# Filling TensorE's first waits with transposes of the identity, and reordering low parts, gathers and up products before the second sequence

## Chip, cores and metric

The kernel runs on one core of one Trainium2 chip. The metric is the device time of one execution in microseconds (us). The core has five engines with their own instruction streams: TensorE (PE; its weight loads are a row of their own, PEld), VectorE (DVE), ScalarE (ACT), GpSimd (POOL) and SyncE (SP, which only issues transfers). Engines wait for one another through semaphores.

## What is computed

The reference is one layer of a language model on 8 sequences of 512 tokens with 128 channels:

```python
h = concat(fine_embed[ids], softmax(cluster[ids] + b) @ coarse)          # token embedding
h = h + attn(layernorm(h))    # rms norm, linear attention with a decay mask, then a gelu "memory" step
h = h + ffn(layernorm(h))     # 2 shared and 64 routed experts, top 6 of 64 per token, 64 hidden units each
# an expert: silu(x @ gate.T) * (x @ up.T) @ down.T, times the token's gate value
```

A token past an expert's capacity gets a gate of zero there, so the kernel needs a running count over the tokens of all sequences.

## The kernel before

The work goes sequence by sequence (`BATCHES` = 8, called b), each in two parts. The first part (the *early* and *late* steps: embedding, attention, router) makes the normalised tokens x3 and the gates of a sequence. The second part runs all experts on all tokens, two experts at a time: `PAIRS` = 33 pairs, p = 0 to 32. For a pair, `gate_up` issues six matmuls of 128x512 (gate and up, each as hi*hi, hi*lo and lo*hi of weights split in two fp32r parts), ACT applies silu (`act_silu`), DVE multiplies by the up product (`dve_up`), POOL multiplies by the gates (L998, or L1002 for pair 0), and four pairs later `down` multiplies by the down weights into one PSUM bank. For odd pairs ACT and DVE also split the hidden values (`act_hi`, `dve_lo`).

The order on each engine is written out by hand. While the experts of sequence b run, the steps of sequence b+1 (late) and b+2 (early) are interleaved: the tables `PE_AT`, `DVE_AT`, `ACT_AT` and `POOL_AT` say at which pair p a step is issued. Before the first sequence nothing can be interleaved, so the same tables are run through without pairs: the *start* of the kernel is a chain of small steps that go from engine to engine. Its steps are: products of the small weights ("prep", L506 to L530), the coarse embedding of sequence 0 (L431, L437), transposes of xn (L343), y (L349 to L351), z and scores (L360 to L362), state (L370), mem (L378, L381), transposes of xn2 (L388), vals (L394), op (L400), transposes of x3 (L406), router logits (L411), the top 6 on DVE, and transposes of the gates (L419). Then DVE counts the tokens of each expert (L795), makes the gates (L800), and SP stores them to DRAM and reads them back as one row per expert, spread over 64 partitions (`gate_row_loads`, L293).

The expert weights come in six chunks of 11 pairs (`CHUNKS`); for each, ACT rounds to the hi part (`split_hi`) and DVE subtracts to get the lo part (`split_lo`, L272). The last number of a chunk's tuple says at which step DVE does it: below `PAIRS` in the start, from `PAIRS` on within the first sequence. `DOWN_LO_AT` is the same for the down weights (L277). Some buffers of later steps serve as staging for these chunks (`hid`, `gate_rows`, `later`).

Token rows are fetched by `gather` on POOL (indirect transfers): those of sequences 0 and 1 at the beginning, those of sequence b+2 between the pairs 1 to 4 of sequence b. `POOL_AT["hx"]` is an addition of 128x512 on POOL (L971) that DVE's h2 (L719) needs much later.

```python
for p in range(PAIRS):
    if p == PE_AT["gates_t"]:
        ...
        for k in range(AHEAD):
            gate_up(pe, 0, 0, k)
    pe_late(pe, 0, 0, p, False)
    pe_early(pe, 1, p - SHIFT, bank_y)
sequences(pe, lambda *a: pe_sequence(pe, *a))
```

Of the kernel before, what the change touches and what calls it, by code (L numbers as in the profile page):

```python
# [29 lines left out]
P = 128  # L30
BATCHES, SEQ = 8, 512
TILES = SEQ // P
# [15 lines left out]
SPLITS = PAIRS // 2  # L48
DOWN_HI_AT, DOWN_LO_AT = 10, PAIRS + 1

# [23 lines left out]
CHUNKS = (("gate", 0, "hid0", None, -20, 3),  # L74
          ("up", 0, "rows", None, -20, 10),
          ("gate", CHUNK, "hid1", None, 3, 14),
          ("up", CHUNK, "later", None, 5, 14),
          ("gate", 2 * CHUNK, "own0", None, 5, PAIRS + 6),
          ("up", 2 * CHUNK, "own1", None, 7, PAIRS + 9))
CHUNK_OF = {(n, p0): k for k, (n, p0, *_) in enumerate(CHUNKS)}  # L80
SHIFT = 3
AHEAD = 2


def build(nc, ids, table, coarse_w, square_w, small_cols, small_rows, gate_t, up_t, down_t, out):
    ctx = ExitStack()
    with ctx:
# [397 lines left out]
        def pe_sequence(pe, b, par, late, early):  # L485
            first = b == 0
            for p in range(PAIRS):
# [10 lines left out]
                if early:  # L498
                    pe_early(pe, b + 2, p)

        @block.tensor
        def _(pe):
            f0, f1 = bank_f

            pe.wait_ge(sem("squares"), 16)
            pe.matmul(f0[:, 0:P], small_w["q"][:, :], small_w["k"][:, :], start=True, stop=True)  # L506
            pe.matmul(f0[:, P:2 * P], small_w["v"][:, :], small_w["o"][:, :], start=True, stop=True,
                      skip_group_check=True)
            pe.matmul(f0[:, 2 * P:3 * P], small_w["read"][:, :], basis[:, :], start=True, stop=True,
                      skip_group_check=True)  # L510
            pe.matmul(f0[:, 3 * P:4 * P], small_w["write"][:, :], basis[:, :], start=True, stop=True,
                      skip_group_check=True).then_inc(sem("pe_prep"), 1)

            pe.wait_ge(sem("ident"), 2)
            pe.wait_ge(sem("powers"), 3)
            pe.transpose(bank_g[0][:, 0:P], mask_t[:, :], ident[:, :])
            pe.matmul(bank_g[0][:, P:2 * P], to_end[:, :], ident[:, :], start=True, stop=True, skip_group_check=True)
            pe.matmul(bank_g[0][:, 2 * P:2 * P + 1], powers_t[:, :], ident[:, 0:1], start=True, stop=True,
                      skip_group_check=True).then_inc(sem("pe_powers"), 1)
            pe.wait_ge(sem("prep1"), 1)  # L520
            pe.matmul(f1[:, 0:P], qk_in[:, :], basis[:, :], start=True, stop=True)
            pe.matmul(f1[:, P:2 * P], vo_in[:, :], basis[:, :], start=True, stop=True,
                      skip_group_check=True).then_inc(sem("pe_prep"), 1)
            pe.wait_ge(sem("coarse_w"), 16)
            for p in range(PAIRS):
                pe_early(pe, 0, p, bank_y)
            pe.wait_ge(sem("prep2"), 1)
            pe.matmul(f0[:, 0:P], qk_t[:, :], basis[:, :], start=True, stop=True, skip_group_check=True)
            pe.matmul(f0[:, P:2 * P], vo_t[:, :], basis[:, :], start=True, stop=True, skip_group_check=True)
            pe.matmul(f0[:, 2 * P:3 * P], read_s[:, :], small_w["mix"][:, :], start=True, stop=True,  # L530
                      skip_group_check=True).then_inc(sem("pe_prep"), 1)
            pe.wait_ge(sem("prep3"), 1)
            pe.wait_ge(sem("cols"), 16)
            for p in range(PAIRS):
                if p == PE_AT["gates_t"]:
                    pe.wait_ge(sem("x3_hi"), 1)
                    pe.wait_ge(sem("x3_lo"), 1)
                    for k in range(AHEAD):
                        gate_up(pe, 0, 0, k)
                pe_late(pe, 0, 0, p, False)  # L540
                pe_early(pe, 1, p - SHIFT, bank_y)
            sequences(pe, lambda *a: pe_sequence(pe, *a))
            last = BATCHES - 1
            for p in range(PAIRS - LAG, PAIRS):
                down(pe, last, 1, p)
            pe_out(pe, last)
# [315 lines left out]
        def dve_sequence(dve, b, par, late, early):  # L862
            first = b == 0
            for p in range(PAIRS):
# [6 lines left out]
                if first:  # L871
                    split_lo(dve, PAIRS + p)
                dve_up(dve, b, par, p)
                if p >= SPLIT_LAG and is_split(p - SPLIT_LAG):
# [5 lines left out]
        def _(dve):  # L880
# [57 lines left out]
            dve.wait_ge(sem("decays"), 3)  # L938
            for p in range(PAIRS):
                dve_late(dve, 0, 0, p)  # L940
                dve_early(dve, 1, 1, p - SHIFT, 1, bank_y)
                split_lo(dve, p)
# [18 lines left out]
        def pool_late(pool, b, par, p):  # L961
# [7 lines left out]
            if p == POOL_AT["hx"]:  # L969
                pool.wait_ge(sem("x2"), b + 1)  # L970
                pool.tensor_tensor(hx[:, :, :], emb[par][:, :, :], x2[:, :, :], ALU.add).then_inc(sem("hx"), 1)  # L971
# [10 lines left out]
        def pool_sequence(pool, b, par, late, early):  # L982
            for p in range(PAIRS):
                if late:
                    pool_late(pool, b + 1, 1 - par, p)
                if early:
                    pool_early(pool, b + 2, p)
                    if p in GATHER_AT:

                        gather(pool, b + 2, par, GATHER_AT.index(p))  # L990
# [15 lines left out]
        def _(pool):  # L1006
# [17 lines left out]
            for p in range(PAIRS):  # L1024
                pool_late(pool, 0, 0, p)
                pool_early(pool, 1, p - SHIFT)
            sequences(pool, lambda *a: pool_sequence(pool, *a))

# [50 lines left out]
```

## Time and profile before

| | us |
|---|---|
| median of 3 runs (lowest, highest) | 728.99 (728.93, 729.01) |
| the profiled execution, its own time | 728.14 |
| its span, first to last instruction | 726.3 |
| TensorE busy in the span | 683.9 (94%) |
| DVE / ACT / POOL busy | 525.2 / 349.5 / 464.8 |

The page shows engines' busy time, a strip of 40 slices of some 18 us each, the chain of work that ended last, and groups of instructions. TensorE's clock as granted is given in shares of full speed (1.00 is 2.4 GHz, 0.50 is 1.2 GHz). In the strip TensorE is below nine tenths only in the first five slices and in the last one:

```profile
PE   4547899999999999999999999999999999999997
PEclk8566999999999999999999999999999999999999
```

### The profile page before, as it was taken

The page shows a single profiled execution, that of the slowest core. Times are in us where ns is not written, and L with a number is a line of the kernel's source. Part 1 is how long each engine was busy: PE and PEld are TensorE (multiplying, and loading weights), DVE is VectorE, ACT ScalarE, POOL GpSimd, SP SyncE. Part 2 cuts the span into 40 slices and gives each one's busy share as a digit, 9 for nine tenths or more (in the row PEclk, how much of TensorE's full clock was granted, in tenths as well). Part 3 has the DMA queues.
Part 4 walks back from the last instruction along what each step waited for, and adds up shares of the span by engine and source line. Part 5 has one row for each costly group of instructions (what it writes and reads, how often), then busy time and mean ns, then how long its engine had stood idle before and what let it go on. Part 6 is the DMA issues. An engine that isn't in the chain of part 4 may idle for free.

```text
span 726.3 us, 9592 instructions
## 1 busy us (share of the span) xinstructions
PE 683.9 (94%) x2943; PEld 512.9 (71%) x2943; DVE 525.2 (72%) x1073; ACT 349.5 (48%) x607; POOL 464.8 (64%) x345
## 2 busy tenths in 40 slices
PE   4547899999999999999999999999999999999997
PEld 3426677777777777777777777777777777777775
DVE  4477877787769877788679877788678866674443
ACT  3333374545554474544654465533745445534432
POOL 5013667685676776676776856777676656676664
PEclk8566999999999999999999999999999999999999
DMA  5501333343333433333333433333334334444431
GB/s 202 221 1 44 112 102 99 116 120 105 116 102 94 131 103 102 116 116 110 109 110 95 131 98 106 115 115 109 107 99 118 115 98 115 107 118 122 138 122 55
DMA packets 48851, 80.14 MB, mean 110 GB/s; under 512 B 9504, under 2 KB 13728, under 8 KB 48800
## 3 DMA queue, kind: packets, MB, share of 16 engines
q1 hardware_dynamic: 47776, 77.44, 34.7%
q0 software_dynamic: 1024, 2.10, 1.4%
q8 instruction: 23, 0.38, 0.2%
q14 instruction: 28, 0.23, 0.1%
HBM read 76.35 MB, written 3.15 MB: 109 GB/s over the span
## 4 chain that ended last, share of the span: by engine, by line
PE 90%; DVE 4%; issue 1%; POOL 1%; ACT 1%; DVEq 0%; POOLq 0%
PE bank_y L459 16%; PE bank_g L473 8%; PE bank_u L475 8%; PE bank_g L475 8%; PE bank_u L474 8%; PE bank_u L473 8%; PE bank_g L474 8%; PE bank_y L454 4%; PE bank_y L456 4%; PE bank_y L453 4%; PE bank_f L378 1%; PE bank_f L394 1%; PE bank_f L411 1%; PE bank_f L400 1%; PE bank_f L370 1%
## 5 line engine op out<-in xcount | busy, mean ns | idle before, releaser
L998 POOL TENSOR_TENSOR hid<-hid,gate_rows 128x512 f32<-128x512 f32 x256 | 374.0, 1470 | 190.1 <-DVE hid L848 189.2
L596 ACT ACTIVATE hid<-bank_g 128x512 f32<-128x512 f32 x264 | 156.4, 598 | 268.2 <-PE bank_g L475 265.5
L848 DVE TENSOR_TENSOR hid<-hid,bank_u 128x512 f32<-128x512 f32 x264 | 178.5, 681 | 131.2 <-PE bank_u L475 78.3
L473 PE MATMUL bank_g<-x_hi,gate_hi 128*128 128x512 f32 x264 | 143.7, 544 | 0.0
L459 PE MATMUL bank_y<-hid,w_down 128*128 128x512 f32 x272 | 138.8, 592 | 0.0
L854 DVE TENSOR_TENSOR hid_lo<-hid,hid_hi 128x512 fp32r<-128x512 f32 x128 | 111.2, 869 | 1.6 <-ACT hid_hi L602 1.5
L475 PE MATMUL bank_g<-x_lo,gate_hi 128*128 128x512 f32 x264 | 105.4, 399 | 0.0
L475 PE MATMUL bank_u<-x_lo,up_hi 128*128 128x512 f32 x264 | 105.3, 399 | 0.0
L474 PE MATMUL bank_g<-x_hi,gate_lo 128*128 128x512 f32 x264 | 105.0, 398 | 0.0
L473 PE MATMUL bank_u<-x_hi,up_hi 128*128 128x512 f32 x264 | 105.0, 398 | 0.0
L474 PE MATMUL bank_u<-x_hi,up_lo 128*128 128x512 f32 x264 | 104.7, 397 | 0.0
L602 ACT ACTIVATE hid_hi<-hid 128x512 fp32r<-128x512 f32 x128 | 80.4, 628 | 5.6 <-POOL hid L998 5.2
L473 PEld LDWEIGHTS bank_g<-x_hi,gate_hi 128*128 128x128 f32 x264 | 50.6, 192 | 24.2 <-issue 19.2
L474 PEld LDWEIGHTS bank_g<-x_hi,gate_lo 128*128 128x128 f32 x264 | 50.7, 192 | 23.6 <-issue 19.2
L459 PEld LDWEIGHTS bank_y<-hid,w_down 128*128 128x128 f32 x272 | 51.2, 188 | 12.0
L474 PEld LDWEIGHTS bank_u<-x_hi,up_lo 128*128 128x128 f32 x264 | 50.1, 190 | 12.1
L473 PEld LDWEIGHTS bank_u<-x_hi,up_hi 128*128 128x128 f32 x264 | 50.2, 190 | 11.9
L475 PEld LDWEIGHTS bank_u<-x_lo,up_hi 128*128 128x128 f32 x264 | 50.0, 190 | 11.9
L475 PEld LDWEIGHTS bank_g<-x_lo,gate_hi 128*128 128x128 f32 x264 | 50.2, 190 | 11.6
L453 PE MATMUL bank_y<-hid_hi,down_hi 128*128 128x512 f32 x128 | 51.1, 399 | 0.0
L456 PE MATMUL bank_y<-hid_lo,down_hi 128*128 128x512 f32 x128 | 50.9, 398 | 0.0
L454 PE MATMUL bank_y<-hid_hi,down_lo 128*128 128x512 f32 x128 | 50.9, 398 | 0.0
(199 smaller groups left out, 828.1 us busy)
## 6 DMA issues: line engine op xcount, KB each, us to landing
gate_rows<-gates_dram SPq DMA_DIRECT2D x512, 128.0 KB, 2.9
w_down<-down_t_dram SPq DMA_DIRECT2D x3, 704.0 KB, 14.0
out_dram<-later SPq DMA_DIRECT2D x8, 256.0 KB, 3.0
hid<-gate_t_dram SPq DMA_DIRECT2D x2, 704.0 KB, 5.8
gates_dram<-gates_t SPq DMA_DIRECT2D x8, 128.0 KB, 2.2
gate_rows<-up_t_dram SPq DMA_DIRECT2D x1, 704.0 KB, 5.7
later<-up_t_dram SPq DMA_DIRECT2D x1, 704.0 KB, 8.6
raw<-gate_t_dram SPq DMA_DIRECT2D x1, 704.0 KB, 9.5
```

What stands on the lines that cost most here:

```text
L453: pe.matmul(y, down_hi[:, j, :], hid_hi[:, k, :], start=False, stop=False)
L454: pe.matmul(y, down_lo[:, j, :], hid_hi[:, k, :], start=False, stop=False)
L456: pe.matmul(y, down_hi[:, j, :], hid_lo[:, k, :], start=False, stop=False).then_inc(sem("down_done"), 1)
L459: pe.matmul(y, w_down[:, p, :], hid[:, slot(par, p), :], start=(p == 0), stop=(p == PAIRS - 1)).then_inc(sem("down_done"), 1)
L473: pe.matmul(o, w_hi[name][:, p, :], x3_hi[par][:, :], start=True, stop=False)
L474: pe.matmul(o, w_lo[name][:, p, :], x3_hi[par][:, :], start=False, stop=False)
L475: pe.matmul(o, w_hi[name][:, p, :], x3_lo[par][:, :], start=False, stop=True).then_inc(sem("pe_" + name), 1)
L596: act.activation(hid[:, slot(par, p), :], bank_g[(p + par) % 2][:, :], ACT.Silu).then_inc(sem("silu"), 1)
L602: act.activation(hid_hi[:, (p // 2) % SPLIT_RING, :], hid[:, slot(par, p), :], ACT.Copy)\
L848: dve.tensor_tensor(hid[:, s, :], hid[:, s, :], bank_u[(p + par) % 2][:, :], ALU.mult)\
L854: dve.tensor_tensor(hid_lo[:, k, :], hid[:, slot(par, p), :], hid_hi[:, k, :].bitcast(F32), ALU.subtract)\
L998: pool.tensor_tensor(hid[:, s, :], hid[:, s, :], gate_rows[:, row, :], ALU.mult)\
```

## The change

TensorE gets extra transposes of the identity (`warm`): each reads `ident` and writes a PSUM bank that nobody reads then. They stand behind steps of the start, in counts that a table gives (20 before anything else, then 2, 9, 4, 26 in the preparation, and 8, 12, 9, 7, 36, 3, 2, 24, 4, 20, 6 behind later steps), in front of the waits that follow these steps. The rest of the change is another order:

- DVE's lo parts: up chunk 0 at step 7 (was 10), gate chunk 1 at step 10 (was 14), up chunk 1 within the first sequence (pair 5; was step 14 of the start), down at step 14 of the start (was pair 1 of the first sequence), the last two chunks at pairs 9 and 12 (were 6 and 9).
- `AHEAD` 3: three pairs' gate and up products are issued ahead of the first sequence, the third behind the transposes of the gates. DVE multiplies pair 0 ahead of the count of tokens and pair 1 right behind the gates, before xn of sequence 1.
- POOL: the gathers of sequence 2 stand before the first sequence; hx of sequence 0 waits for xn2 instead of x2.

```diff
-DOWN_HI_AT, DOWN_LO_AT = 10, PAIRS + 1
+DOWN_HI_AT, DOWN_LO_AT = 10, 14
...
-          ("up", 0, "rows", None, -20, 10),
-          ("gate", CHUNK, "hid1", None, 3, 14),
-          ("up", CHUNK, "later", None, 5, 14),
+          ("up", 0, "rows", None, -20, 7),
+          ("gate", CHUNK, "hid1", None, 3, 10),
+          ("up", CHUNK, "later", None, 5, PAIRS + 5),
...
-AHEAD = 2
+AHEAD = 3
+WARM = {1: 8, 3: 12, 5: 9, 6: 7, 7: 36, 12: 3, 14: 2, 17: 24, 20: 4, PE_AT["gates_t"]: 6}
+WARM_START, WARM_PREP, WARM_EXP, WARM_COARSE, WARM_GATES = 20, (2, 9), 4, 26, 20
...
+        def warm(pe, bank, count):
+            for _ in range(count):
+                pe.transpose(bank[:, 0:P], ident[:, :], ident[:, :])
...
+            pe.wait_ge(sem("ident"), 2)
+            warm(pe, bank_u[1], WARM_START)
             pe.wait_ge(sem("squares"), 16)
...
+            warm(pe, bank_u[1], WARM_COARSE)
             pe.wait_ge(sem("prep3"), 1)
             pe.wait_ge(sem("cols"), 16)
             for p in range(PAIRS):
                 if p == PE_AT["gates_t"]:
                     pe.wait_ge(sem("x3_hi"), 1)
                     pe.wait_ge(sem("x3_lo"), 1)
-                    for k in range(AHEAD):
+                    for k in range(AHEAD - 1):
                         gate_up(pe, 0, 0, k)
+                    warm(pe, bank_y[1], WARM_GATES)
                 pe_late(pe, 0, 0, p, False)
+                if p == PE_AT["gates_t"]:
+                    gate_up(pe, 0, 0, AHEAD - 1)
                 pe_early(pe, 1, p - SHIFT, bank_y)
+                warm(pe, bank_y[1] if p >= PE_AT["gates_t"] else bank_u[1], WARM.get(p, 0))
...
             for p in range(PAIRS):
+                if p == DVE_AT["taken"]:
+                    dve_up(dve, 0, 0, 0)
                 dve_late(dve, 0, 0, p)
+                if p == DVE_AT["taken"]:
+                    dve_up(dve, 0, 0, 1)
...
             if p == POOL_AT["hx"]:
-                pool.wait_ge(sem("x2"), b + 1)
+                pool.wait_ge(sem("x2" if b else "xn2"), b + 1)
...
-                    if p in GATHER_AT:
+                    if p in GATHER_AT and b:
...
+            for t in range(TILES):
+                gather(pool, 2, 0, t)
             sequences(pool, lambda *a: pool_sequence(pool, *a))
```

Where the order moves, on the engines that wait or are waited for. In all rows the first column is the line (lines of the changed kernel are some 4 to 24 higher), and `x36` means 36 in a row.

TensorE between mem (L378, L381; now L382, L385) and the transposes of xn2 (L388; now L392), the last rows of mem included. Before:

```order
L378 MATMUL bank_f<-z,shared 128x128
L381 MATMUL bank_f<-turns 128x128
L378 MATMUL bank_f<-z,shared 128x128
L388 MATMUL bank_f<-ident,xn 128x128 x4
L394 MATMUL bank_f<-xn_t,read_mix 128x512
L431 MATMUL bank_y<-ident,lg 64x128 x4
```

and with the change:

```order
L382 MATMUL bank_f<-z,shared 128x128
L385 MATMUL bank_f<-turns 128x128
L382 MATMUL bank_f<-z,shared 128x128
L508 MATMUL bank_u<-ident 128x128 x36
L392 MATMUL bank_f<-ident,xn 128x128 x4
L508 MATMUL bank_u<-ident 128x128 x3
L398 MATMUL bank_f<-xn_t,read_mix 128x512
L435 MATMUL bank_y<-ident,lg 64x128 x4
```

36 transposes of the identity stand in the longest wait of the start, three more in the next one.

VectorE from the gates' last product (L786; now L805) on: the count and the gates (L795, L800; now L814, L819), the up products of the first pairs (L848; now L867), and the lo part of the down weights (L277). Before:

```order
L786 TENSOR_TENSOR turns<-turns 128x4x64
L795 SCALAR_TENSOR_TENSOR taken<-ones_row,bank_f 64x512
L800 SCALAR_TENSOR_TENSOR gates_t<-taken,bank_f 64x512
L664 TENSOR_SCALAR xn<-emb,mv,inv 128x128 x4
L848 TENSOR_TENSOR hid<-hid,bank_u 128x512
L277 TENSOR_TENSOR down_lo<-w_down,down_hi 128x2048
L848 TENSOR_TENSOR hid<-hid,bank_u 128x512
L679 TENSOR_TENSOR x_lo<-bank_f,x_hi 128x512
```

and with the change, with the stretch further on where the lo part of up chunk 1 now stands (L276):

```order
L805 TENSOR_TENSOR turns<-turns 128x4x64
L867 TENSOR_TENSOR hid<-hid,bank_u 128x512
L814 SCALAR_TENSOR_TENSOR taken<-ones_row,bank_f 64x512
L819 SCALAR_TENSOR_TENSOR gates_t<-taken,bank_f 64x512
L867 TENSOR_TENSOR hid<-hid,bank_u 128x512
L683 TENSOR_SCALAR xn<-emb,mv,inv 128x128 x4
L698 TENSOR_TENSOR x_lo<-bank_f,x_hi 128x512
...
L689 TENSOR_SCALAR x<-emb,mv,inv 128x128 x4
L694 TENSOR_SCALAR shared<-xn,decay_cols 128x384
L276 TENSOR_TENSOR up_lo<-later,up_hi 128x1408
L867 TENSOR_TENSOR hid<-hid,bank_u 128x512
```

The long subtraction L277 is gone from between the first pairs; one of 1,408 columns has come in at pair 5.

GpSimd at the beginning of the first sequence: the gathers (DMA emb), pair 0 (L1002; now L1026) and the products with the gate rows (L998; now L1022). Before:

```order
L979 TENSOR_TENSOR inv<-var,neg_half 128x8
L1002 TENSOR_SCALAR hid<-hid 128x512
L958 DMA emb<-table_dram,idx 128x128
L998 TENSOR_TENSOR hid<-hid,gate_rows 128x512
L958 DMA emb<-table_dram,idx 128x128
L998 TENSOR_TENSOR hid<-hid,gate_rows 128x512
```

and with the change:

```order
L1003 TENSOR_TENSOR inv<-var,neg_half 128x8
L982 DMA emb<-table_dram,idx 128x128 x4
L1026 TENSOR_SCALAR hid<-hid 128x512
L1022 TENSOR_TENSOR hid<-hid,gate_rows 128x512 x9
L990 TENSOR_SCALAR ms<-ss 128x4
L992 TENSOR_TENSOR inv<-ms,neg_half 128x4
```

The four gathers stand together, ahead of pair 0.

## Rows read from the trace of the kernel before

**Rows 1.** Windows: us, busy by engine (instructions), TensorE's granted clock, DMA share, GB/s.

```profile
20.00:30.00 10.00, 5.60 (x19) 4.18 (x19) 5.33 (x12) 5.13 (x6) 0.00 (x0) 0.50 0.78 322
...
80.00:90.00 10.00, 8.04 (x38) 6.23 (x37) 8.74 (x14) 1.72 (x4) 5.05 (x4) 0.83 0.30 86
...
300.00:700.00 400.00, 398.80 (x1727) 298.91 (x1726) 293.91 (x578) 195.94 (x346) 273.83 (x196) 1.00 0.38 112
```

**Rows 2.** Timeline of TensorE, start: start, length, what, [idle before, releaser].

```profile
20.75 1.08 PE L343 MATMUL bank_f<-ident,xn 128*128 128x128 f32 x4 [3.98 <-DVE xn L664]
23.34 0.76 PE L349 MATMUL bank_f<-x_hi,qk_hi 128*128 128x512 f32 x1 [1.50 <-DVE x_lo L679]
...
24.33 0.63 PE L351 MATMUL bank_f<-x_lo,qk_hi 128*128 128x512 f32 x1
26.93 0.55 PE L360 MATMUL bank_f<-vo_y_hi,x_hi 128*128 128x256 f32 x1 [1.97 <-DVE turns L685]
...
29.41 0.41 PE L362 MATMUL bank_f<-vo_y_lo,x_hi 128*128 128x256 f32 x1
...
33.35 0.46 PE L378 MATMUL bank_f<-z,shared 128*128 128x128 f32 x2 [1.24 <-DVE turns L702]
...
35.74 0.64 PE L378 MATMUL bank_f<-z,shared 128*128 128x128 f32 x2
41.94 1.11 PE L388 MATMUL bank_f<-ident,xn 128*128 128x128 f32 x4 [5.56 <-DVE xn L713]
...
46.59 1.51 PE L400 MATMUL bank_f<-write_w,vals 128*128 128x128 f32 x8
...
52.81 1.11 PE L406 MATMUL bank_f<-ident,xn 128*128 128x128 f32 x4 [3.69 <-DVE xn L736]
54.62 1.97 PE L411 MATMUL bank_f<-cols,xn_t 128*128 128x64 f32 x8 [0.69 <-ACT xn_t L576]
...
62.88 0.66 PE L419 MATMUL bank_f<-ident,turns 128*128 128x128 f32 x4 [1.38 <-DVE turns L786]
```

**Rows 3.** Timeline of TensorE, first and last of 12 in z of sequence 1.

```profile
77.66 0.36 PE L360 MATMUL bank_f<-vo_y_hi,x_hi 128*128 128x256 f32 x1 [0.46 <-DVE turns L685]
...
79.03 0.28 PE L362 MATMUL bank_f<-vo_y_lo,x_hi 128*128 128x256 f32 x1
```

**Rows 4.** Timeline of VectorE, start and first sequence.

```profile
9.99 0.49 DVE L808 TENSOR_TENSOR lg<-emb,rows 128x256 f32<-128x256 f32 x1 [0.51 <-DMA emb<-table_dram,idx]
...
40.01 1.87 DVE L713 TENSOR_SCALAR xn<-shared,inv 128x128 f32<-128x128 f32 x4 [1.32 <-POOL inv L968]
...
44.58 1.62 DVE L272 TENSOR_TENSOR up_lo<-later,up_hi 128x1408 fp32r<-128x1408 f32 x1
...
51.65 1.11 DVE L736 TENSOR_SCALAR xn<-h,mv,inv 128x128 f32<-128x128 f32 x4 [0.80 <-POOL inv L974]
...
56.17 0.16 DVE L840 TENSOR_SCALAR var<-mv 128x4 f32<-128x4 f32 x1
...
74.13 2.32 DVE L854 TENSOR_TENSOR hid_lo<-hid,hid_hi 128x512 fp32r<-128x512 f32 x1 [1.18 <-ACT hid_hi L602]
...
78.03 3.20 DVE L670 TENSOR_SCALAR x<-emb,mv,inv 128x128 f32<-128x128 f32 x4
```

**Rows 5.** Timeline of ScalarE, ahead of vals of sequence 0.

```profile
44.01 1.28 ACT L573 ACT_TABLE_LOAD   x1
```

**Rows 6.** Timeline of GpSimd, first pairs of sequence 0.

```profile
67.45 3.37 POOL L1002 TENSOR_SCALAR hid<-hid 128x512 f32<-128x512 f32 x1 [9.40 <-DVE hid L848]
71.00 1.09 POOL L958 DMA_INDIRECT emb<-table_dram,idx  x1 [0.18 <-issue]
72.12 1.31 POOL L998 TENSOR_TENSOR hid<-hid,gate_rows 128x512 f32<-128x512 f32 x1
```

**Rows 7.** The tile gate_rows, 60 to 90 us: its transfers (issue length in ns, from where to where) and landing.

```profile
L293 SPq DMA_DIRECT2D gate_rows<-gates_dram x20: 444/596/606, 67.8 to 89.5; - x20
...
DMA to landing us min/median/max: 2.7/3.1/3.5
```

More of the change, by code:

```diff
@@ L74 @@
 CHUNKS = (("gate", 0, "hid0", None, -20, 3),
-          ("up", 0, "rows", None, -20, 10),
-          ("gate", CHUNK, "hid1", None, 3, 14),
-          ("up", CHUNK, "later", None, 5, 14),
-          ("gate", 2 * CHUNK, "own0", None, 5, PAIRS + 6),
-          ("up", 2 * CHUNK, "own1", None, 7, PAIRS + 9))
+          ("up", 0, "rows", None, -20, 7),
+          ("gate", CHUNK, "hid1", None, 3, 10),
+          ("up", CHUNK, "later", None, 5, PAIRS + 5),
+          ("gate", 2 * CHUNK, "own0", None, 5, PAIRS + 9),
+          ("up", 2 * CHUNK, "own1", None, 7, PAIRS + 12))
 CHUNK_OF = {(n, p0): k for k, (n, p0, *_) in enumerate(CHUNKS)}
 SHIFT = 3
-AHEAD = 2
+AHEAD = 3
+WARM = {1: 8, 3: 12, 5: 9, 6: 7, 7: 36, 12: 3, 14: 2, 17: 24, 20: 4, PE_AT["gates_t"]: 6}
+WARM_START, WARM_PREP, WARM_EXP, WARM_COARSE, WARM_GATES = 20, (2, 9), 4, 26, 20
 def build(nc, ids, table, coarse_w, square_w, small_cols, small_rows, gate_t, up_t, down_t, out):
@@ L512, in _ @@
                       skip_group_check=True).then_inc(sem("pe_prep"), 1)
-            pe.wait_ge(sem("ident"), 2)
             pe.wait_ge(sem("powers"), 3)
@@ L519, in _ @@
                       skip_group_check=True).then_inc(sem("pe_powers"), 1)
+            warm(pe, bank_u[1], WARM_PREP[0])
             pe.wait_ge(sem("prep1"), 1)
@@ L523, in _ @@
                       skip_group_check=True).then_inc(sem("pe_prep"), 1)
+            warm(pe, bank_u[1], WARM_PREP[1])
             pe.wait_ge(sem("coarse_w"), 16)
@@ L526, in _ @@
                 pe_early(pe, 0, p, bank_y)
+                if p == PE_AT["exp_t"]:
+                    warm(pe, bank_u[1], WARM_EXP)
             pe.wait_ge(sem("prep2"), 1)
@@ L872, in dve_sequence @@
                     split_lo(dve, PAIRS + p)
-                dve_up(dve, b, par, p)
+                if p >= AHEAD - 1 or not first:
+                    dve_up(dve, b, par, p)
                 if p >= SPLIT_LAG and is_split(p - SPLIT_LAG):
```

## The prediction

> **What bounds the kernel now.** I read the windows of ten microseconds first. From 300 to 700 us TensorE is busy 398.80 of 400 us at granted clock 1.00; nothing in the change touches that stretch, so no gain or loss is to be had there. From 20 to 30 us it is busy 5.60 of 10 us, and its clock is 0.50, the 1.2 GHz level; from 80 to 90 us it still has 0.83 of full clock, that is some 3.4 us at half speed [rows 1]. So all that can move lies in the first 90 us. The timeline of TensorE there shows a chain: a few matmuls, then a wait with a named releaser on DVE or ACT, eight of them in the rows, from 0.69 to 5.56 us [rows 2]. The matmuls of the chain run at half speed because TensorE waits so much, and each is waited for: its length is on the path. VectorE's, ScalarE's and GpSimd's timelines then tell which of the shortened steps meets another bound [rows 4 to 6].
>
> **Prices.** At half clock z (12 matmuls) runs from 26.93 to 29.82 us, 2.89 us [rows 2]. The same 12 at full clock run from 77.66 to 79.31 us, 1.65 us [rows 3]: a factor of 0.57, which I use for the other steps. One 128-column pass costs 0.20 us at half clock (12 passes from 33.35 to 35.74 us) [rows 2], so a filling transpose costs about 0.20 us at half and 0.12 us at full clock (estimate from that factor).
>
> **The change, part by part: the clock.** If the fillers keep TensorE at 2.4 GHz, the gains up to the gates are:
> - First 20 fillers, prep products: nothing. DVE waits for the gathers until 9.99 us anyway [rows 4]. The coarse products behind that long wait I also leave as they are: between -1.5 us (26 fillers at half clock take 5.2, the wait for xn is 3.98 us [rows 2]) and +1.0 (they become full speed). I take 0.
> - Transposes of xn, 1.08 us [rows 2]: 43% of it, 0.46. y, 23.34 to 24.96: 0.70. z: 1.24. State: left at 0. mem, 33.35 to 36.38: 3.03 x 0.43 = 1.30. op, 1.51, whose last part was at full clock: 0.45 instead of 0.65. Transposes of x3, 1.11: 0.48.
> - vals: transposes and matmuls would gain over a microsecond, but ScalarE's table load of 1.28 us [rows 5] stands ahead of vals and behind the exponential of sequence 1, which hangs on DVE. I take 0.1; the upper end is 0.9, see hx below.
> - Router, 1.97 us: DVE is busy with sequence 1 until 56.33 us [rows 4], TensorE was done at 56.59 [rows 2]. Only 0.28.
> - First up product ahead of the count: 0.69 us in a wait of 0.7 us for the transposes of the gates (62.88 + 0.66 [rows 2]): 0.
>
> **The change, part by part: the order in the start.** xn2 (L713) took 1.87 us, the like L736 1.11 [rows 4]: POOL's hx ran beside it. With hx behind xn2: +0.76. The price is that hx now meets DVE's work on the cluster logits of sequence 1, operations on two tiles like L854, which took 2.32 us beside POOL [rows 4]; one POOL operation of some 1.3 us [rows 6], begun after the first of them and in the way of the third, makes vals 0.8 us later than it could be, which is the 0.1 above. The moved lo parts (1.62 us each [rows 4]) lie in waits: up chunk 0 beside mem, which still takes 3.03 - 1.30 = 1.73 us; gate chunk 1 in the 3.6 us of norm steps between mem's end and xn2's start at 40.01; the lo part of down replaces two others ahead of op. Cover gone, each would cost at most its length. The third `gate_up`, six matmuls where y has three (0.92 us), about 1.9 us, lies between the gates' transposes, which end at 63.54 [rows 2], and the landing of the gate rows near 71 (below).
>
> The four gathers (1.09 us each [rows 6]) now run beside the top 6. The row nearest to this is L808, 0.49 us beside gathers at the beginning [rows 4]; a few such delays of under 0.1 make -0.2 us. The other end, one gather waited for in full by each of two steps, is -2.2; it is a rival below.
>
> Sum to the gates: 0.46 + 0.70 + 1.24 + 1.30 + 0.45 + 0.48 + 0.1 + 0.28 + 0.76 - 0.2 = **5.6 us**.
>
> **From the gates to the end of the idle time (83.5 us).** What releases this stretch is POOL. Before, pair 0 took 3.37 us beside the lo part of down, then a gather stood ahead of each product [rows 6]. With both gone, POOL waits for the gate rows instead: they are issued from 67.8 us, the second half-row 0.6 later, and land 2.7 to 3.5 us after issue [rows 7], so at about 71.4. Pair 1 starts 0.7 earlier than its 72.12. The split of pair 1 (L854, 2.32 us behind two POOL instructions) then waits for one only: another 1.0. x1 (L670, 3.20 us against 1.11 when undisturbed [rows 4]) waits for one POOL operation: another 0.8. Against these stands the lo part of up chunk 1, now on DVE's way to the scores: -1.6. Net **+0.9 us**; ends: -1.6 (POOL keeps getting in between) and +2.5 (the lo part hides). xn of sequence 1 comes 0.6 us later behind the second up product, but the gate rows hide that. TensorE still idles 2 to 3 us ahead of state, so I let the low clock after it recur: 0, upper end +1.7, half of its 3.4 us.
>
> **Total** 6.5 us. The profiled execution took 728.14 us, so 721.6; the median of the runs is 0.85 above it, so **722.5 us**.
>
> **Rivals.**
> - *The clock falls back for parts of the start.* For: the wait ahead of the coarse products stays without enough filling, and later fillers may end well ahead of their waits. Then about half of the clock terms (4.6 us) is lost, and the 26 fillers at half clock hold up xn by about 1 us: 6.5 - 2.3 - 1.0 = 3.2, so 725.8 us. Against: the counts fill most of each wait at 0.12 us each (36 x 0.12 = 4.3 of 5.56 - 0.76 = 4.8 us).
> - *Slower: the fillers do not raise the clock and stand in the way.* They are in TensorE's own queue, so whatever of them exceeds the wait delays the next step. At 0.20 to 0.21 us each, against the idle times [rows 2]: 26 before xn +1.5, 8 before y +0.2, 12 before z +0.5, 9 and 7 around state +0.7, 36 before xn2 +2.0, 24 before x3 +1.4, 20 before the gates +2.8: 9.1 us, less 0.9 after the gates: 8.2 slower, 737.2 us. It decides from 5.56/36 = 0.154 us per filler on. For: no row shows transposes of a constant alone lifting the clock. Against: the four transposes at 62.88 took 0.66 us, those at 20.75 took 1.08 [rows 2]; ahead of the faster ones lay the dense work of the router and two pairs, and the fillers make the start as dense.
> - *The gathers hold up the top 6.* Two of its steps, each behind one gather of 1.09 us [rows 6], cost 2.2 instead of 0.2 us: 724.5 us. For: x1 (L670, 3.20 us) had gathers as well as products beside it [rows 4, 6]. Against: L808 beside gathers alone took 0.49 us. The Trainium skill, SBUF — State Buffer, section "Who interferes with whom", has a rule of that kind: tensor_scalar operations of VectorE can take ports that GpSimd shares, for making descriptors too, and the later one blocks for the whole instruction of the other. No row here shows it with a gather alone.
> - *More than forecast:* vals gains its 0.8, and the idle time ahead of state gets too short to lower the clock, +1.7, with a little of the lo part hidden: 719.5 us or less.
> - *Nothing to see:* what is won before the gates is given back by DVE and POOL at the first pairs; against it, TensorE's queue there simply starts earlier as a whole. 728.5 us.
>
> **Chances.** Forecast 0.54, clock in parts 0.17, gathers 0.07, more than forecast 0.11, slower 0.07, nothing 0.04. Under 0.2% (1.5 us) cannot be told from no change. Faster by over that: 0.54 + 0.11 + 0.07 + 0.15 of the 0.17 = 0.87; slower 0.07; the rest, 0.06, same. The forecast's own range is 720 to 725 (bounds of coarse, vals and DVE's part, not all at once); to hold 8 in 10 it takes in the gathers, most of the clock in parts and most of the better case: 718.8 to 726.6.
>
> **What would show it.** Right: granted clock 1.00 in nearly all windows from 15 to 65 us; z near 1.7 us, mem near 1.8 us; xn2 at 1.1 us; the gates' store 5 to 6 us earlier; pair 0 on POOL under 2 us; state of sequence 1 some 6.5 us earlier; the middle unchanged. Wrong: windows at 0.50 with fillers at 0.2 us right ahead of a real step, DVE's logits or top 6 stretched beside POOL by more than a microsecond, or new idle time on TensorE after 85 us.

## The result and the profile after

The change takes 718.5 us (median; 718.02 to 718.78), beside 728.96 (728.69 to 729.01) for the kernel before on the same chip: a ratio of 0.986 with an interval of 0.984 to 0.987. That is 10.5 us faster, 4.0 us more than forecast, and just below the low end of 718.8. The profiled execution took 718.78 us with a span of 717.0; before it was 728.14 and 726.3. So 9.36 us can be followed in the two traces.

Windows of the changed kernel; columns as in [rows 1]:

```profile
20.00:30.00 10.00, 7.83 (x62) 6.82 (x60) 6.73 (x15) 6.93 (x8) 0.00 (x0) 1.00 0.77 316
42.00:44.00 2.00, 2.00 (x14) 1.93 (x14) 1.79 (x11) 0.00 (x0) 0.00 (x0) 0.71 0.00 0
44.00:46.00 2.00, 2.00 (x11) 2.00 (x10) 1.20 (x6) 0.00 (x0) 1.02 (x1) 0.50 0.00 0
80.00:90.00 10.00, 10.00 (x43) 7.51 (x42) 7.43 (x10) 8.15 (x19) 6.25 (x6) 1.00 0.28 95
300.00:700.00 400.00, 398.82 (x1726) 298.84 (x1724) 289.19 (x558) 195.40 (x344) 273.79 (x196) 1.00 0.36 113
```

Between 20 and 30 us the granted clock is now 1.00, not 0.50; between 80 and 90 us it is 1.00, not 0.83, and TensorE has no idle time left there. The one stretch at half speed lies within 42 to 48 us (the window from 46 on, not shown, has 0.93). The middle is unchanged (398.82 of 400 us busy, before 398.80).

Timeline of TensorE in the start; L508 is the filler:

```profile
11.78 0.60 PE L435 MATMUL bank_y<-ident,lg 128*64 128x128 f32 x4 [1.71 <-issue]
...
13.06 1.10 PE L441 MATMUL bank_y<-coarse_sb,z 64*128 64x64 f32 x8 [0.24 <-ACT z L607]
...
19.71 0.63 PE L347 MATMUL bank_f<-ident,xn 128*128 128x128 f32 x4 [1.85 <-DVE xn L683]
...
24.75 0.36 PE L364 MATMUL bank_f<-vo_y_hi,x_hi 128*128 128x256 f32 x1 [0.66 <-DVE turns L704]
...
26.09 0.28 PE L366 MATMUL bank_f<-vo_y_lo,x_hi 128*128 128x256 f32 x1
...
29.89 0.46 PE L382 MATMUL bank_f<-z,shared 128*128 128x128 f32 x2 [0.48 <-DVE turns L721]
...
31.31 0.39 PE L382 MATMUL bank_f<-z,shared 128*128 128x128 f32 x2
31.53 4.09 PE L508 MATMUL bank_u<-ident 128*128 128x128 f32 x36
36.26 0.66 PE L392 MATMUL bank_f<-ident,xn 128*128 128x128 f32 x4 [0.64 <-DVE xn L732]
...
42.57 4.51 PE L508 MATMUL bank_u<-ident 128*128 128x128 f32 x24
46.91 0.60 PE L410 MATMUL bank_f<-ident,xn 128*128 128x128 f32 x4
...
75.37 0.91 PE L374 MATMUL bank_f<-z,shared 128*128 128x128 f32 x6 [2.38 <-issue]
```

Against [rows 2]: z runs from 24.75 to 26.37, 1.62 us, about what it took at full clock in [rows 3] (1.65); mem from 29.89 to 31.70, 1.81; the transposes of xn2 0.66, not 1.11. The 36 fillers take 4.09 us, 0.114 each, and leave 0.64 us of idle time where there were 5.56. The 24 fillers ahead of L410, in the stretch at half speed, take 4.51 us, 0.188 each. L410 has no wait in front of it: it was fillers that it waited for. The eight coarse products (L441) take 1.10 us; before they took 1.97:

```profile
13.23 1.97 PE L437 MATMUL bank_y<-coarse_sb,z 64*128 64x64 f32 x8 [0.68 <-ACT z L588]
```

VectorE's timeline:

```profile
35.33 0.87 DVE L732 TENSOR_SCALAR xn<-shared,inv 128x128 f32<-128x128 f32 x4 [1.32 <-POOL inv L992]
...
37.02 0.92 DVE L833 TENSOR_TENSOR lg<-lg,soft 128x256 f32<-128x256 f32 x1
...
66.76 1.11 DVE L873 TENSOR_TENSOR hid_lo<-hid,hid_hi 128x512 fp32r<-128x512 f32 x1 [2.94 <-ACT hid_hi L621]
...
69.45 2.08 DVE L689 TENSOR_SCALAR x<-emb,mv,inv 128x128 f32<-128x128 f32 x4
...
71.78 1.61 DVE L276 TENSOR_TENSOR up_lo<-later,up_hi 128x1408 fp32r<-128x1408 f32 x1
```

xn2 takes 0.87 us (1.87 in [rows 4], where it was L713), the split of pair 1 1.11 (2.32), x1 2.08 (3.20). The price of hx behind xn2 is that L833 takes 0.92 us (0.43 before, as L814). The lo part of up chunk 1 is new here, and costs its 1.61 us.

ScalarE ahead of vals, then GpSimd's timeline at the first pairs:

```profile
38.42 1.28 ACT L592 ACT_TABLE_LOAD   x1
39.71 0.69 ACT L592 ACTIVATE vals<-bank_f,cols 128x512 f32<-128x512 f32 x1
```

```profile
53.18 0.95 POOL L982 DMA_INDIRECT emb<-table_dram,idx  x1 [0.30 <-issue]
...
56.93 1.51 POOL L1026 TENSOR_SCALAR hid<-hid 128x512 f32<-128x512 f32 x1 [0.31 <-DVE hid L867]
64.80 4.22 POOL L1022 TENSOR_TENSOR hid<-hid,gate_rows 128x512 f32<-128x512 f32 x3 [6.36 <-DMA gate_rows<-gates_dram]
```

As forecast, vals still stands behind the table load of [rows 5]. Pair 0 takes 1.51 us on POOL (3.37 in [rows 6]), and POOL then waits 6.36 us for the gate rows. The chain of work that ended last, between the gates and pair 1, shows nothing but these transfers:

```profile
58.85 2.23 DMA gates_dram<-gates_t
61.09 0.46 SPq L297
61.55 0.04 issue
61.59 3.06 DMA gate_rows<-gates_dram
```

The steps, by the start of the instruction that takes each one's result in the two timelines (us):

| step, and who takes its result | before | after | gained in this step | forecast |
|---|---|---|---|---|
| coarse products, DVE | 15.23 | 14.20 | 1.03 | 0 |
| transposes of xn, ACT | 21.87 | 20.38 | 0.46 | 0.46 |
| y, ACT | 24.99 | 22.81 | 0.69 | 0.70 |
| z, ACT | 29.86 | 26.41 | 1.27 | 1.24 |
| state, DVE | 32.15 | 28.69 | 0.01 | 0 |
| mem, DVE | 36.41 | 31.73 | 1.22 | 1.30 |
| xn2, vals, ACT | 45.84 | 39.71 | 1.45 | 0.86 |
| op, DVE | 48.13 | 41.65 | 0.35 | 0.45 |
| transposes of x3, ACT | 53.97 | 47.55 | -0.06 | 0.48 |
| router, DVE | 56.62 | 49.83 | 0.37 | 0.28 |
| top 6, count, end of the gates | 65.51 | 58.82 | -0.10 | -0.2 |
| **to the gates** | | | **6.69** | **5.6** |
| pair 1 begins, POOL | 72.12 | 64.80 | 0.63 | 0.7 |
| its split ends, DVE | 76.45 | 67.87 | 1.26 | 1.0 |
| x1, lo part, state of sequence 1, DVE | 84.47 | 76.31 | -0.42 | -0.8 |
| x2 of sequence 2, DVE | 172.41 | 163.04 | 1.21 | 0 |
| end of the span | 726.33 | 716.98 | -0.02 | 0 |

### The profile page after: what moved, and what is told of

Read it like the earlier page. It is cut to its first block, busy times and chain, and to the rows that moved or that the text cites. A ratio compares the mean times of both kernels' runs of the same rounds, so it can differ in the third digit from the quotient of the medians.

```text
span 717.0 us, 9975 instructions
## 1 busy us (share of the span) xinstructions
PE 693.6 (97%) x3135; PEld 524.7 (73%) x3135; DVE 523.5 (73%) x1073; ACT 349.2 (49%) x607; POOL 464.3 (65%) x345
## 4 chain that ended last, share of the span: by engine, by line
PE 88%; DVE 3%; issue 3%; POOL 2%; ACT 1%; DMA 1%; SPq 0%; POOLq 0%; DVEq 0%
PE bank_y L463 16%; PE bank_g L477 8%; PE bank_u L479 8%; PE bank_u L477 8%; PE bank_g L479 8%; PE bank_u L478 8%; PE bank_g L478 8%; PE bank_y L458 4%; PE bank_y L460 4%; PE bank_y L457 4%; POOL hid L1022 1%; PE bank_f L404 1%; PE bank_f L382 1%; PE bank_f L441 1%; PE bank_f L374 1%
## 5 line engine op out<-in xcount | busy, mean ns | idle before, releaser
L1022 POOL TENSOR_TENSOR hid<-hid,gate_rows 128x512 f32<-128x512 f32 x256 | 374.4, 1472 | 196.4 <-DVE hid L867 189.2
L867 DVE TENSOR_TENSOR hid<-hid,bank_u 128x512 f32<-128x512 f32 x264 | 178.4, 681 | 127.9 <-PE bank_u L479 77.7
L873 DVE TENSOR_TENSOR hid_lo<-hid,hid_hi 128x512 fp32r<-128x512 f32 x128 | 110.7, 865 | 3.3 <-ACT hid_hi L621 3.3
```

What stands on the lines that cost most here:

```text
L867: dve.tensor_tensor(hid[:, s, :], hid[:, s, :], bank_u[(p + par) % 2][:, :], ALU.mult)\
L873: dve.tensor_tensor(hid_lo[:, k, :], hid[:, slot(par, p), :], hid_hi[:, k, :].bitcast(F32), ALU.subtract)\
L1022: pool.tensor_tensor(hid[:, s, :], hid[:, s, :], gate_rows[:, row, :], ALU.mult)\
```

## Experiments

The diffs are against the changed kernel. Medians stand with the lowest and highest run, ratios (to the kernel before on the same chip) with their interval. Moments are of the profiled executions; e1 is the changed kernel again, profiled without any window below 1.00 between 5 and 700 us, and so the better comparison for them.

**e1_again**, nothing edited.

> The changed kernel once more, unchanged. Theory (where the clock dips depends on how the execution happens to lie against the clock's own control, so a dip moves from run to run): 718.5 within 0.5 us, but the stretch at 0.50 that the first profile had at 42.8 to 46.3 us lies elsewhere or is missing, and the one ahead of state of sequence 1 may be back. Rival (the dips belong to the program): the same time and the same dip at the same place.

Measured: 720.33 us (718.41 to 720.96), ratio 0.988 (0.986 to 0.990). Timeline of TensorE around the place where the first trace had its half speed:

```profile
42.65 2.84 PE L508 MATMUL bank_u<-ident 128*128 128x128 f32 x24
46.41 0.66 PE L410 MATMUL bank_f<-ident,xn 128*128 128x128 f32 x4 [0.92 <-DVE xn L755]
```

The same 24 fillers take 2.84 us and leave 0.92 us of the wait; ACT takes the transposes of x3 at 47.10, 0.45 earlier than in the first trace. The half speed at 42 to 46 us thus comes in one execution and not in another. When it comes, it is at the same place: in the profiles of e7 and e10 too the granted clock is below 1.00 from 42 to 48 us. The time was not as expected: three of the four runs lie 1.8 to 2.5 us above 718.5. All eight runs of the change lie between 718.0 and 721.0, with a median of 718.7. The three slowest have a mean granted clock of 0.994 to 0.995, the other five 0.996 to 0.999.

**e2_order**, the order without the fillers:

```diff
-WARM = {1: 8, 3: 12, 5: 9, 6: 7, 7: 36, 12: 3, 14: 2, 17: 24, 20: 4, PE_AT["gates_t"]: 6}
-WARM_START, WARM_PREP, WARM_EXP, WARM_COARSE, WARM_GATES = 20, (2, 9), 4, 26, 20
+WARM = {}
+WARM_START, WARM_PREP, WARM_EXP, WARM_COARSE, WARM_GATES = 0, (0, 0), 0, 0, 0
```

> The change without any filling transpose: only the other order. Theory (two parts that add up, the clock being the larger): the order alone saves 1.0 at xn2 and about 1.5 between the gates and state, 726.0 us; granted clock 0.50 in most of 13 to 62 us, z of sequence 0 near 2.9 us, mem near 3.0 us. Rival (the order carries the gain, the fillers little): 722 us or less.

Measured: 726.99 us (725.44 to 728.56), ratio 0.997 (0.996 to 0.998), against 729.16 before: 2.2 us. Its windows:

```profile
20.00:30.00 10.00, 5.61 (x19) 4.18 (x19) 5.01 (x10) 5.75 (x8) 0.00 (x0) 0.50 0.78 320
80.00:90.00 10.00, 8.10 (x38) 6.93 (x38) 5.88 (x12) 2.29 (x7) 4.59 (x3) 0.83 0.19 65
```

The gates end at 65.48 us, where they did before (65.51), but the order does gain on the way: from mem's result to vals it takes 8.44 us (36.81 to 45.25), before 9.43 (36.41 to 45.84), the 1.0 us expected of xn2. This execution loses it to the clock, which fell at other places than before. Its state product, then the same one before:

```profile
30.58 1.62 PE L374 MATMUL bank_f<-z,shared 128*128 128x128 f32 x6 [1.38 <-ACT z L579]
```

```profile
31.20 0.91 PE L370 MATMUL bank_f<-z,shared 128*128 128x128 f32 x6 [1.38 <-ACT z L560]
```

State takes 1.62 us instead of 0.91, op 1.99 instead of 1.51; the coarse products, 1.49 instead of 1.97, give some of it back. State of sequence 1 is reached 0.91 us earlier (83.56 against 84.47), and the low clock behind it (0.83) is that of [rows 1].

**e3_fill**, the fillers in the order of before (`AHEAD`, the lo parts, the gathers, hx and the up products put back):

```diff
-DOWN_HI_AT, DOWN_LO_AT = 10, 14
+DOWN_HI_AT, DOWN_LO_AT = 10, PAIRS + 1
...
-AHEAD = 3
+AHEAD = 2
...
-                pool.wait_ge(sem("x2" if b else "xn2"), b + 1)
+                pool.wait_ge(sem("x2"), b + 1)
...
```

> The kernel before with the same fillers at the same places, nothing else changed. Theory: the clock terms alone, coarse 1.0, transposes of xn 0.45, y 0.7, z 1.25, mem 1.2, op 0.4, vals 0.5, router 0.3, together 5.8: 723.2 us; pair 0 on GpSimd still takes 3.4 us. Rival (the order carries the gain): 726 us or more. If the two parts add up, the savings of this run and of the order alone make 10.5 us together; if this run leaves the second stretch low after state, some 1.6 us are missing.

Measured: 722.03 us (721.28 to 722.65), ratio 0.990 (0.989 to 0.992): 7.1 us. The gates end at 59.71, 5.80 us earlier than before; state of sequence 1 is 5.80 earlier too (78.67), so between the two the fillers alone gain nothing. The two parts give 7.1 + 2.2 = 9.3 us, the whole 8.8 (e1, same chip) to 10.5: within the spread they add up.

**e4_no_head**, no fillers ahead of and within the preparation, the 26 ahead of xn kept:

```diff
-WARM_START, WARM_PREP, WARM_EXP, WARM_COARSE, WARM_GATES = 20, (2, 9), 4, 26, 20
+WARM_START, WARM_PREP, WARM_EXP, WARM_COARSE, WARM_GATES = 0, (0, 0), 0, 26, 20
```

> The change without the 35 fillers ahead of the coarse products (20, 2, 9 and 4); the 26 behind them and all later ones stay. Theory (these keep the clock up for the coarse products, a term that the prediction set to nothing): the 8 coarse products take 2.0 instead of 1.1 us, and some of the 26 fillers run at half speed, 719.5 to 720.2 us. Rival (the first fillers buy nothing, the clock there is luck): 718.5 us, the products as before in both.

Measured: 721.04 us (720.3 to 721.59), ratio 0.989 (0.987 to 0.990), 0.8 us above the expected range, in which only some of the 26 fillers ran at half speed. TensorE's timeline:

```profile
13.65 1.96 PE L441 MATMUL bank_y<-coarse_sb,z 64*128 64x64 f32 x8 [0.68 <-ACT z L607]
...
16.98 5.23 PE L508 MATMUL bank_u<-ident 128*128 128x128 f32 x26
22.05 0.60 PE L347 MATMUL bank_f<-ident,xn 128*128 128x128 f32 x4
```

The coarse products take 1.96 us again, as before the change, and DVE has them at 15.65 instead of 14.25 (e1). All 26 fillers take the 0.20 us of half clock and now hold up the transposes of xn: these begin 2.15 us after DVE's xn (19.90), in the change 1.26 (18.45 to 19.71). 1.40 + 0.89 is the 2.29 us by which the gates come later (60.66 against 58.37 in e1), and the end of the span is 2.37 later. So the head fillers carry both the gain on the coarse products and the cover for the next 26.

**e5_hx_early**, hx back behind x2:

```diff
-                pool.wait_ge(sem("x2" if b else "xn2"), b + 1)
+                pool.wait_ge(sem("x2"), b + 1)
```

> The change with hx of sequence 0 waiting for x2 again, as before the change. Theory (the wait on xn2 takes POOL out of the way of xn2 and costs part of it again at the logits of sequence 1): xn2 takes 1.9 instead of 0.9 us, the third logits operation 0.4 instead of 0.9, vals comes 0.5 to 1.0 us later, and so does the end: about 0.7 us slower than the change run beside it or in the call before. Rival (what is won at xn2 is lost at the logits): no difference.

Measured: 719.73 us (719.05 to 721.41), ratio 0.988 (0.987 to 0.990). VectorE's timeline:

```profile
35.54 1.87 DVE L732 TENSOR_SCALAR xn<-shared,inv 128x128 f32<-128x128 f32 x4 [1.31 <-POOL inv L992]
...
38.23 0.42 DVE L833 TENSOR_TENSOR lg<-lg,soft 128x256 f32<-128x256 f32 x1
```

xn2 is 1.00 us longer, L833 0.50 shorter; vals comes 0.63 us later (40.41 against 39.78 in e1), the gates 0.64 (59.01 against 58.37). Of this, 0.14 us stands already at mem (31.94 against 31.80), ahead of hx. So hx's part is 0.5 us, which can be seen in the trace, not in the medians.

**e6_gathers**, the gathers back between the pairs of sequence 0:

```diff
-                    if p in GATHER_AT and b:
+                    if p in GATHER_AT:
...
-            for t in range(TILES):
-                gather(pool, 2, 0, t)
```

> The change with the gathers of sequence 2 back between the pairs 1 to 4 of sequence 0. Theory (the gate rows set pair 1, so a gather ahead of it costs little there, but the split of pair 1 and x1 of sequence 1 again wait behind two POOL instructions): pair 1 at most 1.1 us later, state of sequence 1 about 2 us later, some 2 us slower. Against the gates: the top 6 becomes 0.1 us shorter at most. Rival (gathers beside the top 6 cost as much as they do between pairs): gates 2 us earlier, no difference at the end.

Measured: 722.35 us (720.48 to 723.14), ratio 0.992 (0.990 to 0.993). GpSimd's and then VectorE's timeline:

```profile
64.14 1.27 POOL L1022 TENSOR_TENSOR hid<-hid,gate_rows 128x512 f32<-128x512 f32 x1 [4.93 <-DMA gate_rows<-gates_dram]
65.56 1.00 POOL L982 DMA_INDIRECT emb<-table_dram,idx  x1 [0.15 <-DMA gate_rows<-gates_dram]
66.58 1.28 POOL L1022 TENSOR_TENSOR hid<-hid,gate_rows 128x512 f32<-128x512 f32 x1
```

```profile
66.11 2.31 DVE L873 TENSOR_TENSOR hid_lo<-hid,hid_hi 128x512 fp32r<-128x512 f32 x1 [2.77 <-ACT hid_hi L621]
...
70.00 3.20 DVE L689 TENSOR_SCALAR x<-emb,mv,inv 128x128 f32<-128x128 f32 x4
```

The gates end at 58.33 us without gathers beside the top 6, at 58.37 with them (e1). From the router's result on, it takes 8.88 us without them (from 49.45) and 8.99 with them (from 49.38): four gathers cost 0.11 us there, as expected. Where it comes from shows in one small operation, L789, first in the changed kernel, then in e6:

```profile
53.74 0.38 DVE L789 TENSOR_SCALAR tstat<-tstat 128x4 f32<-128x4 f32 x1
```

```profile
53.36 0.17 DVE L789 TENSOR_SCALAR tstat<-tstat 128x4 f32<-128x4 f32 x1
```

In the changed kernel it begins during the second gather (53.18 to 54.13) and ends with it. Put back between the pairs, the gathers make the split 2.31 us and x1 3.20 again, about the figures of [rows 4], and state of sequence 1 comes 2.1 us later (77.97 against 75.88).

**e7_uplo**, the lo part of up chunk 1 two pairs later:

```diff
-          ("up", CHUNK, "later", None, 5, PAIRS + 5),
+          ("up", CHUNK, "later", None, 5, PAIRS + 7),
```

> The change with the lo part of up chunk 1 at pair 7 instead of pair 5, behind state instead of ahead of the scores. Theory (its 1.6 us lie on VectorE's way to the scores, while TensorE idles): state of sequence 1 about 1.5 us earlier, and as much at the end. Rival (TensorE's order or POOL sets state): no difference, or slower by the wait that it makes at pair 7.

Measured: 718.3 us (717.79 to 719.18), ratio 0.986 (0.985 to 0.988). From the end of the gates to state of sequence 1 it takes 15.90 us (59.04 to 74.94), in e1 17.51 (58.37 to 75.88): 1.6 us less, the length of the lo part. On the span 0.6 is left, for in this execution the gates come 0.67 us later, 0.14 of it ahead of mem and the rest by half speed around 45 us, and some comes back further on.

**e8_down**, the lo part of down back at pair 1 of the first sequence:

```diff
-DOWN_HI_AT, DOWN_LO_AT = 10, 14
+DOWN_HI_AT, DOWN_LO_AT = 10, PAIRS + 1
```

> The change with the lo part of the down weights back at pair 1 of sequence 0. Theory (pair 0 on POOL again takes 3.4 us beside it, but the gate rows set pair 1, so that is hidden; only xn's lo part of sequence 1 is pushed back, which the gate rows hide too): pair 1 at most 0.3 us later, under 0.5 us slower. Rival (moving it is what brought pair 1 forward): pair 1 0.7 us later or more, 1 us slower or more.

Measured: 719.83 us (718.85 to 721.61), ratio 0.988 (0.986 to 0.990). Pair 0 stays at 1.51 us, where 3.4 was expected: the lo part begins at 59.92, when pair 0 is done (57.88). So it is the up product ahead of the count that frees pair 0, not the move of the lo part. Pair 1 begins at 64.00 (64.31 in e1): this move frees nothing, since pair 1 waits for the gate rows. What this execution shows beside that is the clock. TensorE's timeline and then a window of e8:

```profile
74.59 0.91 PE L374 MATMUL bank_f<-z,shared 128*128 128x128 f32 x6 [2.42 <-issue]
```

```profile
76.00:78.00 2.00, 2.00 (x6) 1.54 (x6) 1.40 (x4) 1.11 (x2) 0.73 (x1) 0.50 0.43 135
```

Behind an idle time of 2.42 us the clock falls to 0.50; behind 2.38 us in the change and 2.41 us in e1 it did not. From state of sequence 1 to x2 of sequence 2 this execution takes 88.33 us (75.54 to 163.87), e1 86.76, the change 86.73: 1.6 us lost.

**e9_fill_more**, 38 more fillers in the preparation's second gap and around the transposes of the gates, and 20 new ones ahead of state of sequence 1:

```diff
-WARM = {..., 20: 4, PE_AT["gates_t"]: 6}
-WARM_START, WARM_PREP, WARM_EXP, WARM_COARSE, WARM_GATES = 20, (2, 9), 4, 26, 20
+WARM = {..., 20: 4, PE_AT["gates_t"]: 18}
+WARM_START, WARM_PREP, WARM_EXP, WARM_COARSE, WARM_GATES, WARM_STATE = 20, (2, 23), 4, 26, 32, 20
...
+                if first and p == PE_AT["state"]:
+                    warm(pe, bank_y[1], WARM_STATE)
```

> The change with more fillers in the waits that it leaves: 23 instead of 9 ahead of the coarse products, 32 instead of 20 ahead of the transposes of the gates, 18 instead of 6 behind them, 20 new ones ahead of state of sequence 1. Theory (the spread of the change's runs, 718.0 to 721.0 us, comes from low clock in stretches that are left idle): all runs within about 0.7 us of 718.3, granted clock 1.00 from 6 us on. Rival (the spread has another source, transfers or the runs' own): the same spread, or slower, as the fillers stand ahead of real work.

Measured: 718.83 us (718.53 to 718.98), ratio 0.986 (0.985 to 0.988). The idle time ahead of state shrinks from 2.4 to 0.77 us, the granted clock is 1.00 in the whole of 10 to 90 us, and the four runs lie within 0.45 us (mean clocks 0.998 to 1.000), where e1's lie within 2.55. With more filling these four runs are steadier, hardly shorter than the change's faster ones.

**e10_best**, e7 and e9 together, with 20 instead of 24 fillers ahead of the transposes of x3 and 8 ahead of state:

```diff
-          ("up", CHUNK, "later", None, 5, PAIRS + 5),
+          ("up", CHUNK, "later", None, 5, PAIRS + 7),
...
-WARM = {..., 17: 24, 20: 4, PE_AT["gates_t"]: 6}
-WARM_START, WARM_PREP, WARM_EXP, WARM_COARSE, WARM_GATES = 20, (2, 9), 4, 26, 20
+WARM = {..., 17: 20, 20: 4, PE_AT["gates_t"]: 18}
+WARM_START, WARM_PREP, WARM_EXP, WARM_COARSE, WARM_GATES, WARM_STATE = 20, (2, 23), 4, 26, 32, 8
```

> Both that helped, together: the lo part of up chunk 1 at pair 7, and the waits filled more (23 ahead of the coarse products, 32 and 18 around the transposes of the gates, 8 ahead of state of sequence 1, where less idle time is left; 20 instead of 24 ahead of the transposes of x3). Theory: state of sequence 1 near 74.5 us, 717.4 us with a spread under 0.8. Rival (with the waits filled the two do not add up): 718.3 us or more.

Measured: 717.21 us (717.1 to 718.08), ratio 0.984 (0.983 to 0.986): the best version, 11.4 us below the kernel before and 1.3 below the change's result, on different chips. State of sequence 1 is reached at 74.60, the span ends at 715.62. The spread, 0.98 us, is above the 0.8 expected. The profile has the low stretch at 42 to 46 us again (0.61), but it costs little: the 20 fillers take 4.07 us, and the transposes of x3 begin at 46.47, where behind 24 in the change they begin at 46.91.

**e11_many**, 48 instead of 24 fillers ahead of the transposes of x3:

```diff
-WARM = {..., 17: 24, ...}
+WARM = {..., 17: 48, ...}
```

> The change with 48 instead of 24 fillers ahead of the transposes of x3. Theory (fillers stand in TensorE's own queue, and what exceeds the wait delays the step behind, at 0.107 us each at full clock): the 24 of the change leave about 1.1 us of the wait in a run without low clock there, so 24 more reach 1.5 us too far; transposes of x3 and the end 1.5 us later, 720.2 us beside 718.7. Rival (fillers cost nothing, TensorE passes them over): no difference.

Measured: 721.25 us (720.08 to 721.85), ratio 0.989 (0.988 to 0.991). TensorE's timeline:

```profile
42.58 5.46 PE L508 MATMUL bank_u<-ident 128*128 128x128 f32 x48
47.87 0.60 PE L410 MATMUL bank_f<-ident,xn 128*128 128x128 f32 x4
```

At full clock 48 fillers take 5.46 us, 0.114 each, and the transposes begin 1.46 us later than in e1 (46.41); the gates end 1.41 later. What exceeds the wait is paid in full. This is the mechanism of the slower rival, here at the price of full clock. The span ends 2.8 us later than in e1 (719.4 against 716.6), for behind state the clock fell here too. TensorE's timeline and a window:

```profile
76.16 0.91 PE L374 MATMUL bank_f<-z,shared 128*128 128x128 f32 x6 [2.38 <-issue]
```

```profile
78.00:80.00 2.00, 2.00 (x6) 1.55 (x5) 1.28 (x3) 1.11 (x2) 1.16 (x1) 0.50 0.35 120
```

The idle time is the 2.38 us of the change, where the clock stayed up. From state of sequence 1 to x2 of sequence 2 it takes 88.32 us (77.11 to 165.43), as in e8.

## Why the prediction was right and wrong

The mechanism was right: outside one stretch the granted clock stays at 1.00, and the steps that a next engine waits for get shorter by about the forecast factor. Transposes of xn, y, z, mem, op and router together gained 4.36 us; forecast were 4.43. Pair 1 and its split came as forecast (1.89 for 1.7), and so did the 1.6 us price of the lo part. The forecast's sum was 6.5 us against 9.36 in the traces. The steps that failed:

- **"Coarse products: I take 0."** They gained 1.03 us, the upper of the bounds (-1.5 to +1.0). I left the term at 0 because a long wait stood ahead. Most of that wait is still there (1.71 us ahead of L435, 1.73 before), but with 35 fillers around it the eight products take 1.10 us instead of 1.97, and they start 0.17 earlier. e4 shows both ends: without the head fillers the gain is gone and the 26 fillers cost 0.89.
- **"I let the low clock after it recur: 0, upper end +1.7."** It did not recur in the two profiles of the change, which gained 1.2 us there. In e8 and e11 it did, at the same idle time. The idle time alone does not decide, so a single value was the wrong form: against the kernel before, the stretch from state to x2 of sequence 2 gained 1.2 us without the fall and lost 0.4 with it (88.33 against 87.94).
- **xn2 and vals: 1.45 for 0.86.** xn2 gained 1.00 (0.87 against 1.87), not 0.76: L736, taken from [rows 4] as the undisturbed length (1.11), is a longer form, which also subtracts a mean, and it still takes 1.12 with the change (L755). hx in the way of the logits cost 0.50 (L833), not 0.8. e5 confirms both: 1.87 and 0.42.
- **Gates to state: 1.47 for 0.9.** x1 gained 1.12, not 0.8, and the split 1.26, not 1.0.
- **Transposes of x3: -0.06 for 0.48.** The half speed at 42 to 48 us made the 24 fillers 4.51 us long. e1, without it, is 0.52 us shorter from h2 to here (41.72 to 47.10, against 41.65 to 47.55).
- **The median's 0.85 us above the profiled execution** was carried over from the kernel before. Here the median was 0.28 below it. Three of the change's eight runs took 720.3 to 721.0, though, so by how much the forecast misses depends on which runs are drawn: the four of e1 have a median of 720.33, which would have lain within the range, with the same steps wrong.

The gaps sum to 2.86 us in the traces and 1.13 in the offset, the 4.0 by which the forecast was too high.

The rivals: *nothing to see* and *slower* fell, the second by its deciding price: 0.114 us per filler, below 0.154, save at low clock (0.188 each between 42 and 47 us). *The gathers hold up the top 6* fell (e6: 0.11 us). Between POOL's products it is another matter: there they cost 2.1 us up to state (e6). The Trainium skill, SBUF — State Buffer, section "Who interferes with whom", says that a VectorE instruction with both inputs in SBUF contends with GpSimd instructions that read SBUF. L873 (two such inputs) agrees: 0.68 us when alone, 2.31 in e6, where it begins at 66.11 during a gather and ends at 68.42, past the product that follows (66.58 to 67.86). The rule in the same section of the Trainium skill on tensor_scalar operations and descriptors, named beside the rival, agrees with L789, a tensor_scalar that ends with the gather: 0.38 us instead of 0.17. But L796, another one, takes 0.29 us during the third gather as it does in e6 without one, and none of the top 6 waited for a whole gather. *The clock falls back in parts* happened on a small scale, one stretch of some microseconds in some executions. *More than forecast* is what came, but only in part by its causes. vals gained more, and the clock behind state stayed up; yet the rival wanted a shorter idle time for that, and it grew to 2.38 us. Before the change it was 1.96:

```profile
83.53 0.91 PE L370 MATMUL bank_f<-z,shared 128*128 128x128 f32 x6 [1.96 <-DVE shared L692]
```

So this gain was luck of the executions profiled, as e8 and e11 show. The coarse products the rival did not name.

What stays open: which low stretches make the runs of 720 to 721 us. None of them was profiled, and the mean granted clock goes with the time in the change's eight runs but not everywhere: in e2 the run with 0.992 took 728.56 us and one with 0.966 took 727.01. Two low stretches were seen in profiles: the one at 42 to 48 us, which cost 0.45 us in the first profile, and the one behind state, 1.6 us in e8 and e11. Together they would make 2.0 us, about what lies between the slow runs of e1 and its profiled 718.41; that these two make the slow runs is not shown. e9's narrow spread speaks for low clock in waits that the change leaves unfilled, with four runs only; e10's is wider again.

## What to carry to other kernels

Where a chain of small TensorE steps waits for other engines, count each step at the price of both clocks, and fill the waits from TensorE's first instruction on, so that the later fillers are cheap too; but a filler too many is paid in full, so leave room for the price at half clock, as the 20 of e10 do, or accept it in some runs. On an engine pair that blocks each other, order the work so that the long helper operation of the one meets work of the other that nobody waits for. And where a term depends on the clock behind a borderline wait, give it two values with chances, not one.

## What the runs showed of the hardware that was not expected

- About the same idle time of TensorE ahead of state of sequence 1, 2.38 to 2.42 us, was followed by granted clock 1.00 in four executions (the change, e1, e4, e5) and by 0.50 in two (e8, e11). The shorter 1.96 us before the change was followed by a fall, 1.97 us in e3 was not. The Trainium skill, TensorE: Matmul & The Clock Gate, section "What's actually happening", says that the moment at which the clock changes varies from run to run; in these traces it varies even whether the clock falls at all.
- The half speed at 42 to 46 us lay in a stretch where TensorE was busy throughout (2.00 of 2.00 us), behind waits of 0.36 and 1.07 us; what came before did not look idle. e1 has the same two waits and no fall.
- The recorded clock can read 1.00 over work at half speed: in e4's windows from 10 to 20 us it is 1.00 while eight coarse products take 1.96 us, against 1.10 in the change. The same page of the Trainium skill, section "Seeing it yourself", warns that such records have been unreliable; here the durations are the safer witness.
- Four gathers on GpSimd, 0.94 to 1.07 us each, cost VectorE's top 6 only 0.11 us, though one operation in it was held until a gather's end, while hx beside L833 makes it 0.92 instead of 0.42 us, and a gather with a product behind it makes L873 2.31 instead of 0.68. Which of these two instructions held L873 isn't shown.
